# A two-layer conditioned network on one core: the first block's call re-ordered, and a third feed-forward layer whose rounding moves from VectorE to ScalarE

## The chip, the cores and the metric

The kernel runs on one core of one Trainium2 chip. The metric is the device time of one execution in microseconds (us), taken as the median of three runs. The engines are TensorE (PE in the views, with its weight loads as PEld), VectorE (DVE), ScalarE (ACT), GpSimd (POOL) and SyncE (SP, which here only issues DMAs). Each engine runs its own instructions in order, and they meet through semaphores.

## What is computed

```
x = L0_attn_x                                   # [8 sequences, 512 tokens, 128]
sa, ca, ga, sb, cb, gb = split(silu(L0_c) @ L0_wmod)
h = layernorm(x) * (1 + ca) + sa
x = x + ga * L0_attn(h)     # layernorm(ssm(h @ Wp + bp) @ Wo + bo + h) * gamma + beta
h = layernorm(x) * (1 + cb) + sb
x = x + gb * L0_ffn(h)
    # g = silu(h @ w1 * s1) * (h @ w2 * s2)     128 -> 512
    # g = gelu(g @ h1 * s); g = gelu(g @ h2 * s)  512 -> 512, twice
    # return g @ w3 * s3                        512 -> 128
# then the same with block L1: a gated linear attention, and a mixture of LoRA experts
```

The weights `w1, w2, h1, h2, w3` of the first feed-forward network hold only -1, 0 and 1. `ssm` is a linear recurrence over the 512 tokens with 32 states. Only block L0, the function `front` of the kernel, is touched by the change.

## The kernel before

`front` works on the eight sequences in four pairs. A pair `i` has two slots `s`. Its feed-forward network is 24 tiles `j` (the list `TILES`): `j` 0 to 7 are the gated first layer (two products, `gate` and `up`, for each 128 of the 512 hidden columns and each slot), 8 to 15 the first gelu layer (`k` = 1), 16 to 23 the second gelu layer (`k` = 2, the third layer of the network). A tile of a gelu layer is eight 128x512 matmuls into one PSUM bank: four pieces of the 512 hidden rows, and for each one product with the high part of the activations (`hi`, rounded to the type fp32r) and one with the low part (`lo`, the remainder). L1042 is the product with `hi`, L1043 that with `lo`. Gate, up and gelu results take four of the eight PSUM banks in a ring; the other work takes the rest. `USES` lists, by hand, which result goes into which bank in which order, and `Claims` makes TensorE wait for the reader of what stood there before.

Each engine's program is written out by hand as well, as a loop over `i` and `j` with side work hung in at fixed tiles. For the sequence `b` the side work is the recurrent block, in this order:

- `moments_in(b)` (DVE: mean and variance of x), `rescale` (POOL: power -0.5), `apply` or `normalise` (the normalised x, `ssm_out`)
- `flip_h` (PE: four transposes), `bring_h` (ACT: scale and shift into `ssm_hT`), `project` (PE, one for a pair), `bring_u` (ACT), `scan` (DVE, the recurrence, one for a pair)
- `z` (PE: output projection plus residual), `moments_out` (DVE), `rescale_shift` (POOL), `normalise_z` (ACT), `add_bias` (POOL), `update` (DVE: x is updated)
- `moments_ffn` (DVE), `rescale` (POOL), `apply_ffn` (DVE), `flip_ffn` (PE), `bring_ffn` (ACT, twice: full and rounded), `low_h` (DVE: the low part)

For the first pair all of this stands in `prepare`, ahead of the first tile; the modulation vectors (`vectors`, of `SOON` and of `LATER`), the rows spread over partitions (`make_diag` and `spread`) and the flag stand there too. The flag says whether the weights are exact in fp32r: ScalarE sums the low halves of the weights (`sum_piece`), VectorE and TensorE make one number of it, and TensorE branches on it into `run(True)` (two products for each piece) or `run(False)`. With these inputs the flag is zero.

`w_hi` is the rounded copy of all weights, made by ScalarE in seven pieces (`high_piece`), and `w_lo` the remainder, made by POOL in seven pieces (`low_piece`, L732), which only `run(False)` multiplies with. ScalarE's first gelu tile waits for all seven (`w_low`).

In layer 0 a tile goes: ScalarE `silu` of gate, VectorE `product` (L574), ScalarE `round_product` (L844), VectorE `lower` (L587). In the layer `k` = 1 ScalarE evaluates the gelu twice from PSUM, once into `hi` (L853) and once in full (L855), and VectorE subtracts (L587). In `k` = 2 ScalarE evaluates it once, VectorE copies it into `hi` (L585) and subtracts (L587).

## Time and profile before

| | |
|---|---|
| median of 3 runs | 633.18 us (632.43 to 634.87) |
| profiled execution, its own time | 634.81 us |
| its span | 633.0 us |
| PE busy | 543.7 us (86%) |
| DVE busy | 414.6 us (66%) |
| ACT busy | 325.0 us (51%) |
| POOL busy | 228.0 us (36%) |

The span runs from the first to the last instruction of one profiled execution; what lies around it is 1.8 us. Busy is the sum of an engine's instruction times. The clock column of a view is the granted TensorE clock as a share of full speed (1.00 is 2.4 GHz, 0.50 is 1.2 GHz). `front` fills the stretch from 0 to about 266 us; the second block follows it.

### The profile page before, as it was taken

What the parts mean: (1) busy time and instruction counts of PE and PEld (TensorE: products, weight loads), DVE (VectorE), ACT (ScalarE), POOL (GpSimd) and SP (SyncE); (2) the same over time, 40 slices, a digit from 0 to 9 for tenths busy, and PEclk for the clock granted to TensorE, in tenths of its full rate; (3) what the DMA queues carried; (4) which work ended last, traced back from release to release, by engine and by line L of the source; (5) the groups of instructions that cost most, each with busy time, mean ns of one, the idle gap of its engine ahead of it and who ended that gap; (6) DMA issues with size and microseconds to landing.
All of it is one profiled execution on the core that took longest, in us unless ns stands there. A gap on an engine that the chain in (4) does not pass through costs nothing. (4 is left out here: it accounts for less than half of the span.)

```text
span 633.0 us, 10177 instructions
## 1 busy us (share of the span) xinstructions
PE 543.7 (86%) x3688; PEld 444.2 (70%) x3688; DVE 414.6 (66%) x1065; ACT 325.0 (51%) x573; POOL 228.0 (36%) x268
## 2 busy tenths in 40 slices
PE   3837879999999999849999999999999627999994
PEld 2523657777778777638788888888888526878873
DVE  4588649867878675436696776869677642656732
ACT  3467453884886785357655455555542003343340
POOL 2388454802001000044364726446461431323311
PEclk9958889999999999959999999999999966999997
DMA  8300000000040000000000000000000000010001
GB/s 306 98 2 1 2 1 1 1 1 2 29 133 0 1 1 1 0 2 0 1 3 2 1 2 2 2 1 2 1 2 2 1 0 1 1 34 17 26 26 34
DMA packets 10209, 11.67 MB, mean 18 GB/s; under 512 B 656, under 2 KB 9040, under 8 KB 10032
## 3 DMA queue, kind: packets, MB, share of 16 engines
q1 hardware_dynamic: 9120, 10.50, 5.1%
q8 instruction: 30, 0.49, 0.3%
q10 hardware_dynamic: 1040, 0.52, 0.3%
q14 instruction: 19, 0.16, 0.1%
HBM read 8.92 MB, written 2.10 MB: 17 GB/s over the span
## 5 line engine op out<-in xcount | busy, mean ns | idle before, releaser
L1042 PE MATMUL bank<-ffn_g_hi,w_hi 128*128 128x512 f32 x288 | 118.5, 411 | 0.1
L1043 PE MATMUL bank<-ffn_g_lo,w_hi 128*128 128x512 f32 x288 | 114.7, 398 | 0.0
L1287 DVE TENSOR_TENSOR_SCAN att_decay<-bank,att_ident 128x512 f32<-128x512 f32 x64 | 77.6, 1213 | 35.2 <-PE bank L1599 35.0
L587 DVE TENSOR_TENSOR ffn_g_lo<-ffn_full,ffn_g_hi 128x512 fp32r<-128x512 f32 x96 | 70.7, 736 | 33.6 <-ACT ffn_full L855 32.2
L1607 PEld LDWEIGHTS bank<-att_qT,att_hT 128*128 128x128 f32 x512 | 66.0, 191 | 5.5 <-issue 2.0
L1607 PE MATMUL bank<-att_qT,att_hT 128*128 128x128 f32 x512 | 68.0, 276 | 0.6 <-DVE att_state L1311 0.6
L1042 PEld LDWEIGHTS bank<-ffn_g_hi,w_hi 128*128 128x128 f32 x288 | 54.5, 189 | 15.3 <-issue 2.6
L1043 PEld LDWEIGHTS bank<-ffn_g_lo,w_hi 128*128 128x128 f32 x288 | 54.6, 190 | 13.3 <-issue 1.2
L855 ACT ACTIVATE ffn_full<-bank,cols 128x512 f32<-128x512 f32 x64 | 44.3, 693 | 35.1 <-PE bank L1043 29.2
L1486 ACT COPY att_qT<-bank 128x512 f32<-128x512 f32 x64 | 37.3, 587 | 44.7 <-PE bank L167 41.5
L1295 DVE TENSOR_TENSOR att_prob<-bank,att_decay 128x512 f32<-128x512 f32 x64 | 42.6, 666 | 21.9 <-issue 20.5
L1389 POOL TENSOR_TENSOR att_vw<-att_v,att_decay 128x128 f32<-128x128 f32 x64 | 25.9, 406 | 69.4 <-DVE att_decay L1287 69.4
L1977 PE MATMUL bank<-l,lora_hid 128*128 128x155 f32 x256 | 35.6, 296 | 0.0
L1042 PE MATMUL bank<-ffn_h_hi,w_hi 128*128 128x512 f32 x64 | 29.2, 457 | 7.1 <-ACT ffn_gate L839 3.0
L1977 PEld LDWEIGHTS bank<-l,lora_hid 128*128 128x128 f32 x256 | 34.2, 189 | 0.0
L711 POOL TENSOR_TENSOR ffn_in_rstd<-ffn_in_var,neg_half 128x4 f32<-128x4 f32 x8 | 10.6, 1323 | 63.5 <-DVE ffn_in_var L491 63.5
L853 ACT ACTIVATE ffn_g_hi<-bank,cols 128x512 fp32r<-128x512 f32 x32 | 22.2, 693 | 18.2 <-PE bank L1043 18.0
L1855 POOL TENSOR_TENSOR lora_h_lo<-lora_hT,lora_h_hi 128x512 fp32r<-128x512 f32 x8 | 10.2, 1270 | 57.0 <-DVE lora_h_hi L1776 57.0
L1358 POOL TENSOR_SCALAR att_var<-att_mv 128x4 f32<-128x4 f32 x8 | 1.9, 232 | 73.7 <-DVE att_mv L1267 73.1
L574 DVE SCALAR_TENSOR_TENSOR ffn_full<-bank,cols,ffn_gate 128x512 f32<-128x512 f32 x32 | 23.5, 743 | 6.7 <-ACT ffn_gate L839 6.7
L165 PE MATMUL bank<-att_h_hi,m_hi 128*128 128x512 f32 x64 | 27.8, 434 | 0.0
L1043 PE MATMUL bank<-ffn_h_lo,w_hi 128*128 128x512 f32 x64 | 26.8, 419 | 0.0
(225 smaller groups left out, 1292.6 us busy)
## 6 DMA issues: line engine op xcount, KB each, us to landing
w_raw<-in_w_all SPq DMA_DIRECT2D x1, 2304.0 KB, 13.3
out<-lora_res SPq DMA_DIRECT2D x8, 256.0 KB, 2.3
x<-in_x SPq DMA_DIRECT2D x3, 512.0 KB, 12.6
wmod<-in_wmod SPq DMA_DIRECT2D x1, 768.0 KB, 6.3
stage<-in_sel SPq DMA_DIRECT2D x1, 640.0 KB, 8.5
v_raw<-in_v_all SPq DMA_DIRECT2D x1, 576.0 KB, 6.0
x<-in_x ACTq DMA_DIRECT2D x1, 512.0 KB, 4.5
w_raw<-in_w_all SPq DMA_DIRECT2D x1, 512.0 KB, 7.0
```

The source lines that it names most:

```text
L165: pe.matmul(acc, w[0], x[0], start=start, stop=False)
L574: dve.scalar_tensor_tensor(out=full[j % 4][:, :], in0=bank("up", i, j)[:, :], scalar=r["w_scale"][:, 1, m:m + 1], in1=gate[j % 2][:, :], o ...
L587: dve.tensor_tensor(lo, full[j % 4][:, :], hi.bitcast(F32), ALU.subtract).then_inc(low, 1)
L855: act.activation(full[j % 4][:, :], ps, ACT.Gelu, scale=scale).then_inc(gelu_ready, 1)
L1042: pe.matmul(acc, w[0], x[0], start=start, stop=False)
L1043: return pe.matmul(acc, w[0], x[1], start=False, stop=stop)
L1287: dve.tensor_tensor_scan(decay[at % ND][:, :], bank("decay", b, k)[:, :], ident4[:, :], 0.0, ALU.mult, ALU.add).then_inc(decay_ready, 1)
L1295: dve.tensor_tensor(prob[k][:, :], bank("score", b, k)[:, :], decay[at % ND][:, :], ALU.mult).then_inc(prob_ready, 1)
L1389: pool.tensor_tensor(vw[s][:, :, hs], v[s][:, :, hs], last.broadcast_to([P, T, DV]), ALU.mult).then_inc(vw_ready, 1)
L1486: act.copy(qT[b % 2][:, k, :], bank("q", b, k)[:, :]).then_inc(q_ready, 1)
L1607: mm = pe.matmul(ps[:, cc], hT[s][:, cc], qT[s][:, k, cc], start=True, stop=True)
L1977: mm = pe.matmul(bank_e[s][t // 2][:, at:at + D + AR], hid[s][:, k, t * P:(t + 1) * P], r["war2"][:, k, :], start=(k == 0 and t % 2 == 0), ...
```

## The change

It re-orders the side work of `front`, and does four other things:

- **Third layer.** For `k` = 2, as for `k` = 1, ScalarE evaluates the gelu twice (into `hi` and in full), and VectorE's copy L585 and its wait are gone.
- **No `w_lo`.** POOL's seven subtractions and the waits for them are gone. `run(False)`, which these inputs don't take, multiplies with the raw fp32 weights instead.
- **Setup.** The DMAs come in another order and in smaller pieces; `loaded_cond` no longer covers `wmod`. The sigmoid comes ahead of the silu. For sequences 0 and 1 z is normalised by VectorE (`centre`: subtract the mean, times the gain; `update_centred`: times rstd, plus x) without ScalarE's `normalise_z`. `spread` multiplies a broadcast column with the identity, so `make_diag` is gone. Gates of the later modulations (`gates_later`) move into layer 0. The flag's reduction on VectorE is gone. TensorE makes the `LATER` vectors between `z(0)` and `z(1)`. Only the first sequence is brought to its first tile in `prepare`; `flip_ffn(1)`, `bring_ffn(1)` and `low_h(1)` stand in layer 0.
- **Loop.** The z of the next pair are made at tiles 8 and 9 of the pair before it, no longer a pair earlier; `z(2)` and `z(3)` thus leave layer 0 of the first pair. Normalising x for sequences 2 to 7 goes from POOL (L722) to ScalarE (`normalise`), two of them in `prepare` and four in the gelu tiles. Preparing the second block's constants moves from the third pair into the fourth.

```diff
-                sp.dma_start(cT[:, :, :], d["cT"]).then_inc(loaded_cond, 16)
                 sp.dma_start(r["cols"][:, :], d["cols"]).then_inc(loaded_cols, 16)
...
+                sp.dma_start(rows[:, :], d["rows"]).then_inc(loaded_rows, 16)
+                sp.dma_start(cT[:, :, :], d["cT"]).then_inc(loaded_cond, 16)
+                sp.dma_start(wmod[:, 0, 0:3, :], d["wmod"][:, 0, 0:3, :]).then_inc(loaded_soon, 16)
+                sp.dma_start(r["cols"][:, :], d["cols"]).then_inc(loaded_cols, 16)
+                load_w(0)
+                load_x(1)
+                load_w(1)
+                load_w(2)
+                sp.dma_start(wmod[:, 0, 3:6, :], d["wmod"][:, 0, 3:6, :]).then_inc(loaded_later, 16)
+                sp.dma_start(wmod[:, 1, :, :], d["wmod"][:, 1, :, :]).then_inc(loaded_later, 16)
...
+                def centre(b):
+                    dve.wait_ge(spread_ready, 1)
+                    for t in range(T):
+                        ins = dve.scalar_tensor_tensor(out=zn[b][:, t, :], in0=bank("z", b)[:, t * P:(t + 1) * P], scalar=n_out["mv"][:, b, t, 0:1], in1=r["gain_attn0"][:, b, :], op0=ALU.subtract, op1=ALU.mult)
+                    ins.then_inc(centred, 1)
+
+                def update_centred(b):
+                    dve.wait_ge(n_out["rstd_ready"], b + 1)
+                    dve.wait_ge(centred, b + 1)
+                    dve.wait_ge(biased, b + 1)
+                    for t in range(T):
+                        ins = dve.scalar_tensor_tensor(out=x_of(b)[:, t, :], in0=zn[b][:, t, :], scalar=n_out["rstd"][:, b, t:t + 1], in1=x_of(b)[:, t, :], op0=ALU.mult, op1=ALU.add)
+                    ins.then_inc(updated, 1)
...
                     hi, lo = (hid[s][k % 2][q][:, m, :] for q in range(2))
                     if k == 0:
                         dve.wait_ge(high, products(i, j))
-                    elif k == 1:
-                        dve.wait_ge(gelu_ready, gelus(i, j))
                     else:
                         dve.wait_ge(gelu_ready, gelus(i, j))
-                        dve.tensor_copy(hi, full[j % 4][:, :]).then_inc(rounded, 1)
-                        dve.wait_ge(rounded, i * N0 + j - 2 * N0 + 1)
                     dve.tensor_tensor(lo, full[j % 4][:, :], hi.bitcast(F32), ALU.subtract).then_inc(low, 1)
...
-                def low_piece(k):
-                    pool.wait_ge(w_high, k + 1)
-                    pool.tensor_tensor(r["w_lo"][:, piece(k)], w_raw[:, piece(k)], r["w_hi"][:, piece(k)].bitcast(F32), ALU.subtract).then_inc(w_low, 1)
...
+                def normalise(b):
+                    act.wait_ge(n_in["shift_ready"], b - 1)
+                    act.wait_ge(mm, full_at("flip", b - 2))
+                    for t in range(T):
+                        ins = act.activation(ssm_out[b % 2][:, t, :], x_of(b)[:, t, :], ACT.Identity, scale=n_in["rstd"][:, b, t:t + 1], bias=n_in["shift"][:, b, t:t + 1])
+                    ins.then_inc(in_normed, 1)
...
                     ps, scale = bank("gelu", i, j)[:, :], r["w_scale"][:, 1 + k, m:m + 1]
-                    if k == 1:
-                        if i == 0 and j == N0:
-                            act.wait_ge(w_low, PIECES)
-                        act.activation(hid[s][1][0][:, m, :], ps, ACT.Gelu, scale=scale)
+                    act.activation(hid[s][k % 2][0][:, m, :], ps, ACT.Gelu, scale=scale)
                     act.wait_ge(low, made(i, j - 4))
                     act.activation(full[j % 4][:, :], ps, ACT.Gelu, scale=scale).then_inc(gelu_ready, 1)
...
+                        if i < 3:
+                            if j in (11, 12):
+                                normalise_z(e + j - 11)
+                            if j in (18, 19):
+                                bring_ffn(e + j - 18)
+                        if i < 2:
+                            if j in (14, 20):
+                                normalise(e + 2 + (j == 20))
+                            if j in (16, 22):
+                                bring_h(e + 2 + (j == 22))
+                            if j == 23:
+                                bring_u(i + 2)
...
+                            if i < 3 and j in (8, 9):
+                                z(claim, e + j - 8)
+                            if i == 0 and j in (11, 12):
+                                spread(claim, j - 9)
+                            if i < 2 and j == 15:
+                                flip_h(claim, e + 2)
+                            if i < 3 and j in (17, 18):
+                                flip_ffn(claim, e + j - 17)
+                            if i < 2 and j == 21:
+                                flip_h(claim, e + 3)
+                            if i < 2 and j == 23:
+                                project(claim, i + 2)
```

In the last two pieces `e` is `2 * i + 2`, the first sequence of the next pair.

The first place is VectorE in the setup, from the flag's number (`w_inexact`) to the low part of the first layer's input (`ffn_h_lo`). Before:

```order
L635 TENSOR_SCALAR w_inexact<-bank 1x1
L554 TENSOR_TENSOR ssm_zn<-ssm_zn,gain_attn 128x512
L557 TENSOR_TENSOR x<-x,ssm_zn 128x512
L483 BN_STATS ffn_in_stats<-x 128x6 x4
L487 BN_AGGR ffn_in_mv<-ffn_in_stats 128x2 x4
L490 TENSOR_SCALAR ffn_in_neg<-ffn_in_mv 128x4
L491 TENSOR_SCALAR ffn_in_var<-ffn_in_mv 128x4
L508 TENSOR_SCALAR ffn_out<-x,ffn_in_mv,ffn_in_rstd 128x128 x8
L542 TENSOR_TENSOR stage<-cols,spread_col 128x512 x2
L562 TENSOR_TENSOR ffn_h_lo<-ffn_h,ffn_h_hi 128x512 x2
```

And in the changed kernel:

```order
L629 TENSOR_SCALAR w_inexact<-bank 1x1
L479 BN_STATS ssm_out_stats<-bank 128x6 x4
L483 BN_AGGR ssm_out_mv<-ssm_out_stats 128x2 x4
L488 TENSOR_SCALAR ssm_out_var<-ssm_out_mv 128x4
L505 TENSOR_SCALAR ffn_out<-x,ffn_in_mv,ffn_in_rstd 128x128 x4
L555 SCALAR_TENSOR_TENSOR ssm_zn<-bank,ssm_out_mv,gain_attn 128x128 x4
L563 SCALAR_TENSOR_TENSOR x<-ssm_zn,ssm_out_rstd,x 128x128 x4
L479 BN_STATS ffn_in_stats<-x 128x6 x4
L483 BN_AGGR ffn_in_mv<-ffn_in_stats 128x2 x4
L488 TENSOR_SCALAR ffn_in_var<-ffn_in_mv 128x4
L578 TENSOR_TENSOR ffn_h_lo<-ffn_h,ffn_h_hi 128x512
L505 TENSOR_SCALAR ffn_out<-x,ffn_in_mv,ffn_in_rstd 128x128 x4
```

The second sequence's output moments now stand here, and one of the two `ffn_h_lo` stands ahead of the second sequence's `apply_ffn`.

The second place is TensorE at the start of the program. Before, up to the first z (L979 and L980):

```order
L991 MATMUL bank<-scT,wmod 128x8 x3
L241 MATMUL bank<-cols,ssm_out 128x128 x8
L1019 MATMUL bank<-rows 64x128
L1022 MATMUL bank<-cols 32x1 x2
L991 MATMUL bank<-scT,wmod 128x8 x9
L970 MATMUL bank<-ssm_hT,cols 32x512 x2
L986 MATMUL bank<-ffn_full,ones 128x512 x2
```

And in the changed kernel, up to the first z:

```order
L964 MATMUL bank<-scT,wmod 128x8 x3
L990 MATMUL bank<-rows 64x128
L994 MATMUL bank<-cols 32x1 x2
L241 MATMUL bank<-cols,ssm_out 128x128 x8
L938 MATMUL bank<-ssm_hT,cols 32x512 x2
L958 MATMUL bank<-cols,spread_col 128x128 x8
```

The nine `LATER` vectors have left the place ahead of the projection, and the two spreads are eight 128x128 products instead of two 128x512 ones.

The third place is ScalarE at tiles 12 to 16 of the first pair. Before (tiles 12 to 16 are the last of five single L855, with two L853 ahead of them):

```order
L853 ACTIVATE ffn_g_hi<-bank,cols 128x512
L855 ACTIVATE ffn_full<-bank,cols 128x512
L795 ACTIVATE ssm_hT<-bank,sa_bo,mod 128x512
L853 ACTIVATE ffn_g_hi<-bank,cols 128x512
L855 ACTIVATE ffn_full<-bank,cols 128x512
L853 ACTIVATE ffn_g_hi<-bank,cols 128x512
L855 ACTIVATE ffn_full<-bank,cols 128x512
L801 ACTIVATE ssm_u<-bank,b_bias,rows 64x512
L853 ACTIVATE ffn_g_hi<-bank,cols 128x512
L855 ACTIVATE ffn_full<-bank,cols 128x512 x5
```

And in the changed kernel, around tiles 14 to 16:

```order
L770 COPY bias_attn<-bank 128x512
L746 ACTIVATE ssm_out<-x,ssm_in_shift,ssm_in_rstd 128x128 x4
L815 ACTIVATE ffn_g_hi<-bank,cols 128x512
L817 ACTIVATE ffn_full<-bank,cols 128x512
L815 ACTIVATE ffn_g_hi<-bank,cols 128x512
L817 ACTIVATE ffn_full<-bank,cols 128x512
L758 ACTIVATE ssm_hT<-bank,sa_bo,mod 128x512
```

The four short L746 stand between the gelus of tile 14 and tile 15, and the pairs of gelus go on through the third layer.

## Rows read from the trace of the kernel before

**Rows 1.** Stretches: length, busy PE, PEld, DVE, ACT, POOL, clock, DMA, GB/s.

```profile
44.20:70.70 26.50, 19.62 (x76) 13.95 (x77) 23.78 (x46) 18.00 (x27) 19.99 (x11) 0.79 0.00 1
70.70:118.50 47.80, 42.18 (x196) 32.59 (x195) 31.83 (x115) 26.23 (x49) 28.07 (x28) 0.96 0.00 1
118.50:169.20 50.70, 49.50 (x238) 38.73 (x237) 39.34 (x98) 35.91 (x59) 10.62 (x11) 1.00 0.00 1
169.20:215.50 46.30, 45.29 (x209) 36.06 (x208) 36.20 (x79) 34.92 (x54) 2.90 (x2) 1.00 0.17 56
```

**Rows 2.** The timeline of the setup: start, length, engine, line, operation, idle before it.

```profile
8.54 0.22 ACT L860 ACTIVATE scT<-cT 128x16 f32<-128x16 f32 x1 [6.01 <-DMA wmod<-in_wmod]
...
11.11 2.14 DVE L508 TENSOR_SCALAR ssm_out<-x,ssm_in_mv,ssm_in_rstd 128x128 f32<-128x128 f32 x8
...
15.17 4.01 PE L991 MATMUL bank<-scT,wmod 128*128 128x8 f32 x18
...
19.11 1.92 PE L970 MATMUL bank<-ssm_hT,cols 128*32 128x512 f32 x4
...
20.96 3.78 PE L986 MATMUL bank<-ffn_full,ones 128*128 128x512 f32 x4
...
22.05 1.22 DVE L548 TENSOR_TENSOR_SCAN ssm_state<-lam_col,ssm_u 64x512 f32<-64x512 f32 x1 [3.42 <-ACT ssm_u L801]
...
24.54 0.43 PE L979 MATMUL bank<-cols,ssm_hT 128*128 128x128 f32 x2
...
26.57 0.89 DVE L483 BATCH_NORM_STATS2 ssm_out_stats<-bank 128x6 f32<-128x128 f32 x4 [2.20 <-PE bank L980]
...
34.38 0.87 DVE L483 BATCH_NORM_STATS2 ffn_in_stats<-x 128x6 f32<-128x128 f32 x4
...
35.85 0.14 DVE L635 TENSOR_SCALAR w_inexact<-bank 1x1 int32<-1x1 f32 x1
...
40.80 1.94 PE L241 MATMUL bank<-cols,ffn_out 128*128 128x128 f32 x8 [9.37 <-DVE ffn_out L508]
...
44.28 0.77 PE L1042 MATMUL bank<-ffn_h_hi,w_hi 128*128 128x512 f32 x1 [1.54 <-issue]
```

**Rows 3.** One DMA of the start: size in KB, us from issue to landing.

```profile
rows<-in_rows SPq DMA_DIRECT2D x1, 48.8 KB, 3.9
```

**Rows 4.** The timeline of the first pair's layer 0: DVE and POOL.

```profile
60.31 6.73 POOL L732 TENSOR_TENSOR w_lo<-w_raw,w_hi 128x768 fp32r<-128x768 f32 x3
60.53 2.16 DVE L587 TENSOR_TENSOR ffn_g_lo<-ffn_full,ffn_g_hi 128x512 fp32r<-128x512 f32 x1
...
62.61 2.82 DVE L548 TENSOR_TENSOR_SCAN ssm_state<-lam_col,ssm_u 64x512 f32<-64x512 f32 x1
```

**Rows 5.** The timeline of PE where the first gelu tiles of the first two pairs begin.

```profile
65.48 0.72 PE L979 MATMUL bank<-cols,ssm_hT 128*128 128x128 f32 x2 [4.08 <-DVE ssm_state L548]
...
70.71 0.48 PE L1042 MATMUL bank<-ffn_g_hi,w_hi 128*128 128x512 f32 x1
...
130.63 0.48 PE L1042 MATMUL bank<-ffn_g_hi,w_hi 128*128 128x512 f32 x1
...
132.58 0.40 PE L1042 MATMUL bank<-ffn_g_hi,w_hi 128*128 128x512 f32 x1
```

**Rows 6.** PE's waits from 70 to 120 us: total, times, longest.

```profile
PE bank L241 <- POOL ssm_out L722: 3.5, 1, 3.5
PE bank L979 <- DVE ssm_state L548: 1.3, 1, 1.3
```

**Rows 7.** Groups of front's instructions: busy, mean ns, idle before, releasers.

```profile
L587 DVE TENSOR_TENSOR ffn_g_lo<-ffn_full,ffn_g_hi 128x512 fp32r<-128x512 f32 x96 | 70.7, 736 | 33.6 <-ACT ffn_full L855 32.2
...
L855 ACT ACTIVATE ffn_full<-bank,cols 128x512 f32<-128x512 f32 x64 | 44.3, 693 | 35.1 <-PE bank L1043 29.2 <-DVE ffn_g_lo L587 5.9
...
L585 DVE CAST ffn_g_hi<-ffn_full 128x512 fp32r<-128x512 f32 x32 | 13.7, 428 | 15.1 <-ACT ffn_full L855 15.0
```

**Rows 8.** One stretch after that wait of 3.5 us, columns as in rows 1.

```profile
82.70:86.10 3.40, 3.40 (x12) 2.60 (x11) 0.00 (x0) 0.48 (x1) 3.40 (x5) 0.50 0.00 0
```

More of the change, by code:

```diff
@@ L1120, in _ @@
+                    y(PAIRS - 1, 1)
+                    for b in (B - 2, B - 1):
+                        flip_y(claim, b)
                 claim = Claims()
```

580 lines of the change are left out of this document (256 added, 324 removed).

## The prediction

> **What bounds the kernel now.** I read the stretches first, cut where a pair's first tile begins on TensorE [rows 1]. From the second pair on, TensorE is busy for 49.50 of 50.70 us and 45.29 of 46.30: there it is the bound, and what the other engines save is worth nothing as long as they keep up. The two stretches ahead of that are different. From 44.20 to 70.70, the first pair's layer 0, TensorE is busy for 19.62 of 26.50 us, at a mean clock of 0.79, while VectorE is busy for 23.78. The first pair's gelu tiles, 70.70 to 118.50, hold idle time too. And before 44.28 no product of the feed-forward network has started at all [rows 2]. The second block follows, and the change does not touch it. So I look for the gain in three places ahead of 118.50, and for losses in what TensorE has to do or to wait for behind it.
>
> The setup was read in the timeline, as a chain backwards from 44.28 [rows 2]. The reader is to see: the silu waits 6.01 us for the DMA of `wmod`; the nine LATER vectors take 4.01 us on TensorE ahead of the projection; z starts at 24.54; z's first bank is read at 26.57, 2.0 us later; then two sequences go one after the other through VectorE, POOL and ScalarE, up to the transposes at 40.80.
>
> **The setup, step by step.** (a) The silu no longer waits for `wmod`. It now stands behind the sigmoid, which needs `rows`; that DMA is issued first and takes 3.9 us [rows 3], so nothing can be earlier than about 4.6. I take 6.5 for the silu, between 4.6 and 8.54: minus 2.0, bounds minus 3.9 and 0. (b) The LATER vectors leave the place ahead of the projection: minus 3.9 (they fill TensorE's queue from 15.17 to 19.11, and the projection behind them could have run). (c) The first sequence's `apply` (1.07 us, half of L508's 2.14) now stands ahead of the modulations instead of behind them and the gates, so the transposes start sooner: minus 1.4, by that `apply` and a little of the gates; bounds 0 and minus 2.1. Between the projection and z nothing gets shorter: the two spreads hold TensorE for 3.8 us, from 20.96, which is longer than `bring_u` and the scan (over at 23.27). The eight 128x128 products that replace them stream the same number of columns. So z(0) starts at 24.54 - 2.0 - 3.9 - 1.4 = 17.2.
>
> (d) From there I count forward. z(0) 2.0, to 19.2. VectorE: moments 1.5 (34.38 to 35.85), to 20.7, then `centre`. It has no row; four 128x128 operations of the same engine, as in `apply`, are 1.07 us, and I take 1.1 for it and for `update_centred`, with the two passes they replace as the other bound (1.4 together for 128x512 twice; so 0.7 to 1.4 each). That gives 21.8. Meanwhile TensorE makes the LATER vectors, 4.0 us as in the row, or half of it if the clock is up by then; I take 3.0, to 22.2, and VectorE waits for them. Modulations 0.2 (two operations like the 0.14 of 35.85), `update_centred` 1.1, moments 1.5: 25.0. The flag's number and the second sequence's moments 1.6: 26.6. `apply_ffn(0)` 1.1: 27.7. The second sequence's centre, update and moments 3.7: 31.4. `low_h(0)` 0.7, a subtraction like L587 [rows 7]: 32.1. Transposes and `bring_ffn` go beside it: from 40.80 to 44.28 they took 3.5 us with `low_h` in it, so 2.8 without; from 27.7 they are over at 30.5, ahead of `low_h`. The first product then starts at about 32, against 44.28: **minus 12.2**, bounds minus 9 and minus 14.5. TensorE's branch is the one cost without a row: the flag is written at 35.85 and the transposes start at 40.80, so it is anywhere from 0 to 4.9 us. With 4.9 the first product would be at 33.3, which lies within the bounds.
>
> **Layer 0 of the first pair.** Before it takes 26.4 us (44.28 to 70.71). Two things leave it. z(2) and z(3) fill TensorE from 65.48 to 70.71, 5.2 us [rows 5], and they were waited for (4.08 us, for a scan). And POOL's subtractions are gone. The rows show what these did [rows 4]: while L732 ran, a subtraction took 2.16 us and the scan 2.82, where the same subtraction has a mean of 0.74 over the whole of `front` [rows 7] and the scan took 1.22 in the setup [rows 2]. What comes in: `bring_ffn(1)` on ScalarE, `low_h(1)` and `gates_later` on VectorE (0.7, and six operations on few columns, at 0.14 to 0.2 each about 1). Four of five pieces of `w_hi` go out. For the result I take the nearest whole layer: the second pair's runs from 118.50 to 130.63, 12.1 us, with no `low_piece` beside it [rows 1, 5]. To that I add ScalarE's extra work that it lacks (at the 0.69 us of a 128x512 evaluation [rows 7]: `bring_ffn` 1.4, two `bring_h` 1.4, `bring_u` 0.7, a piece of 768 columns 1.0 in proportion, less one `bring_y` 0.7: 3.8), and take off 0.9, a part of what TensorE spent there on output products of the pair before: 15.0. So **minus 11.4**; bounds 13 us and 18 us for the layer, the upper one if TensorE, which starts it after an idle stretch, runs most of it at the lower clock level.
>
> The Trainium skill, page "SBUF — State Buffer", section "Who interferes with whom", bears on this: a VectorE instruction with two SBUF inputs, or in a mode with two ports, is blocked for the whole of a GpSimd instruction that reads SBUF. By this rule the long VectorE instructions go with L732, and the layer falls as above. Without it they'd stay long, and the layer would only lose its 5.2 us of z.
>
> **The first pair's gelu tiles**, 47.8 us. Gone are the waits of 3.5 us for POOL's normalise and of 1.3 us for a scan [rows 6] and the stretch at half clock that followed the first, 3.40 us at 0.50, which costs 1.7 [rows 8]. The z of sequences 4 and 5 are replaced by those of 2 and 3, even. New waits: `flip_h` stands after tiles 15 and 21, and `normalise` on ScalarE behind the gelus of 14 and 20. After the tile's end ScalarE needs two evaluations (1.3 us) and four of 128x128. These have no row for x as the input; together they are at least one 128x512 evaluation, 0.7, and at most four, 2.8; I take 1.5, nearer to the lower end as the columns are the same. So 2.8 us, while the next tile gives TensorE 1.9 us of work (130.63 to 132.58) [rows 5]: 0.9 us of wait each, bounds 0.1 and 2.2, and in the first pair 0.7 more for a `spread`; the projection after tile 23 waits 0.3 more. Together 2.8. z(2) may wait up to 1 for its scan; I take 0.4. Sum: -6.5 + 3.2 = **minus 3.3**.
>
> **Behind it.** The third pair gets two z that it did not have: **plus 3.6** (1.8 each: the first one's 2.0 in the setup, less the handing over to its reader). The second pair gets the same waits of `normalise`: **plus 2.2**. The constants' work moves from the third to the fourth pair, even. The double gelu: 32 more evaluations, at 0.69 us or a little less where they follow each other, on ScalarE, 32 copies of 0.43 us off VectorE [rows 7]. In the second pair ScalarE is busy for 35.91 of 50.70 us; with 8 more gelus (5.5) and two `normalise` (3.0) it is at 44.4. It fits, so I cost it at nothing; TensorE's products hide it. If that cover went, each would cost up to 0.69, 22 in all.
>
> **The sum.** -12.2 - 11.4 - 3.3 + 3.6 + 2.2 = -21.1. The profiled execution took 634.8 us, which is 1.6 above the median; I take the difference to the median, 633.2 - 21.1 = 612.1, and forecast 612.
>
> **Rivals.**
> - *More in front* (0.09): the silu near 4.6, LATER at the higher clock and layer 0 in 13 us: -2, -1 and -2 more, and TensorE never waits for `normalise` because it lags anyway (-4): about 603.
> - *VectorE stays slow in layer 0* (0.10). The long instructions might come from something else than L732, or layer 0 now ping-pongs between three engines with TensorE at half clock. Then the layer loses only z, 21.2 us instead of 15.0: 618. For it speaks that the new layer holds more side work of ScalarE; against it, that the long ones all lie beside POOL's spans.
> - *The setup hardly gains* (0.06). LATER's DMA now stands behind all weights in SP's queue and has no row; before, the whole of `wmod` had landed at 8.54 from the fourth place. If it came at 24 instead of before 19, all that follows would be 5 later: 617, with layer 0's trouble 622.
> - *Slower than before* (0.03): ScalarE becomes the bound of the gelu tiles. The place is the wait for tile j-4's reader on TensorE's ring. It decides when ScalarE needs over 1.9 us a tile throughout: at 1.3 and an average of 0.5 of side work it is at 1.8, so that idle time and then the half clock of rows 8 would come in. A gelu tile at half clock is 1.9 us longer; from 12 of the 64 on, the gain is gone, and with 24 the time is about 657.
> - *The change doesn't do what it says* (0.01): the flag sends TensorE into the fp32 branch. In that type a 128x512 product takes 0.9 us and more (3.78 us for the two spreads [rows 2]) where the gelu tiles have eight in 1.9: some 700 products would be 0.7 us longer each, and the time over 1,000. It sums the same low halves as before, so nothing speaks for it.
>
> **Chances.** The forecast itself, 605 to 617, gets 0.71. The range of 603 to 619 holds it and the near halves of the first three rivals. What a measurement of this kernel can tell from no change is about 0.5%, 3.2 us. Faster by more than that: 0.95; within it 0.01, from the edge of the third rival; slower 0.04, from the last two.
>
> **What the new profile would show.** The silu's ACTIVATE near 6.5; the first z near 17; the first 128x512 product near 32; the first gelu product near 47, and no VectorE instruction of over 1.5 us beside it; waits of about 1 us of the transposes L241 for `ssm_out` from ScalarE, four of them, in place of the 3.5 from POOL; pair starts of TensorE about 91, 144 and 194; the last product of `front` near 245 instead of 266. I am wrong if TensorE waits for ScalarE in the third layer, if the first z waits for LATER's DMA, or if the clock column falls in the gelu tiles.

## The result, and the profile after

The changed kernel takes 619.1 us (median of 4 runs, 618.3 to 619.4) where the kernel before, on the same chip, takes 634.0 (632.4 to 635.5): a ratio of 0.976, 95% interval 0.973 to 0.979. The forecast was 612, with a range up to 619. So the direction and most of the size were right, but the time is 7 us above the forecast, at the very edge of the range. The profiled execution took 619.1 us with a span of 616.8, against a span of 633.0 before: 16.2 less.

The stretches of the changed kernel, from the first product of each pair to that of the next (columns as in [rows 1]; the first line is the setup, the second the first pair's layer 0, the third its gelu tiles, then the second, third and fourth pairs, and the second block):

```profile
0.00:30.90 30.90, 15.54 (x100) 12.09 (x101) 22.72 (x119) 19.07 (x30) 12.93 (x22) 0.91 0.64 208
...
30.90:44.90 14.00, 13.08 (x48) 9.11 (x49) 11.99 (x23) 11.07 (x19) 2.29 (x2) 0.83 0.00 1
44.90:89.20 44.30, 40.93 (x205) 32.40 (x205) 28.93 (x94) 36.91 (x66) 11.24 (x12) 1.00 0.00 1
89.20:145.80 56.60, 51.67 (x237) 39.55 (x236) 37.43 (x107) 43.09 (x75) 10.70 (x12) 0.97 0.00 1
145.80:197.20 51.40, 47.67 (x225) 37.71 (x224) 34.17 (x87) 38.18 (x64) 5.55 (x6) 1.00 0.15 50
197.20:250.60 53.40, 51.50 (x249) 40.94 (x247) 26.85 (x40) 42.10 (x68) 0.00 (x0) 1.00 0.00 1
250.60:616.80 366.20, 317.79 (x2683) 271.28 (x2680) 227.00 (x556) 157.35 (x298) 146.36 (x188) 0.94 0.02 7
```

Against [rows 1] the first pair is far shorter (layer 0 by 12.4, the gelu tiles by 3.5), but the second pair is 5.9 us longer, and TensorE is now idle in it for 4.9 us where before it was idle for 1.2. The third grew by 5.0 (from 46.4 to 51.4 by TensorE's starts), the fourth by 2.6.

The setup on ACT, PE and DVE (columns as in [rows 2]):

```profile
5.76 0.22 ACT L825 ACTIVATE scT<-cT 128x16 f32<-128x16 f32 x1
...
6.54 1.42 PE L964 MATMUL bank<-scT,wmod 128*128 128x8 f32 x6 [6.54 <-DMA wmod<-in_wmod]
...
10.75 1.96 PE L938 MATMUL bank<-ssm_hT,cols 128*32 128x512 f32 x4
12.64 2.05 PE L958 MATMUL bank<-cols,spread_col 128*128 128x128 f32 x16
15.03 0.46 PE L947 MATMUL bank<-cols,ssm_hT 128*128 128x128 f32 x2 [0.34 <-issue]
...
17.88 2.17 PE L964 MATMUL bank<-scT,wmod 128*128 128x8 f32 x18 [0.83 <-DMA wmod<-in_wmod]
...
22.85 0.14 DVE L629 TENSOR_SCALAR w_inexact<-bank 1x1 int32<-1x1 f32 x1
...
24.31 1.11 DVE L505 TENSOR_SCALAR ffn_out<-x,ffn_in_mv,ffn_in_rstd 128x128 f32<-128x128 f32 x4
...
27.52 1.09 PE L241 MATMUL bank<-cols,ffn_out 128*128 128x128 f32 x4 [5.36 <-issue]
...
30.92 0.77 PE L1019 MATMUL bank<-ffn_h_hi,w_hi 128*128 128x512 f32 x1 [2.31 <-issue]
```

The first product starts at 30.92 instead of 44.28. TensorE's waits from 45 to 262 us, in which the changed loop lies (columns as in [rows 6]; a wait of 8.5 us that belongs to the second block is left out):

```profile
...
PE bank L241 <- ACT ssm_out L746: 6.9, 4, 1.8
PE bank L1019 <- ACT ffn_gate L804: 2.7, 3, 0.9
PE bank L241 <- DVE ffn_out L505: 2.4, 1, 2.4
```

Four waits of `flip_h` for ScalarE's `normalise` have taken the place of the one for POOL [rows 6], as forecast in number, but at 1.5 to 1.8 us and not 0.9. The view counts a wait from the modelled end of the last product, and products overlap by 0.15 us; what TensorE loses is 0.15 more, and from here on I call that the gap: 1.66, 1.99, 1.83 and 2.00 us for the four. A wait of 2.4 us for VectorE in `flip_ffn`, in the third pair, was not forecast. Here is what ScalarE does ahead of the last of the four (timeline of ACT; L815 and L817 are the two gelus, L247 `bring_ffn`, L746 `normalise`), and TensorE's answer:

```profile
129.19 0.69 ACT L815 ACTIVATE ffn_g_hi<-bank,cols 128x512 fp32r<-128x512 f32 x1 [1.34 <-PE bank L1020]
129.78 0.68 ACT L817 ACTIVATE ffn_full<-bank,cols 128x512 f32<-128x512 f32 x1
130.35 0.78 ACT L247 ACTIVATE ffn_h_hi<-bank,mod 128x512 fp32r<-128x512 f32 x1
131.01 0.79 ACT L247 ACTIVATE ffn_h<-bank,mod 128x512 f32<-128x512 f32 x1
131.68 0.70 ACT L815 ACTIVATE ffn_g_hi<-bank,cols 128x512 fp32r<-128x512 f32 x1
132.25 0.71 ACT L817 ACTIVATE ffn_full<-bank,cols 128x512 f32<-128x512 f32 x1
132.82 0.81 ACT L247 ACTIVATE ffn_h_hi<-bank,mod 128x512 fp32r<-128x512 f32 x1
133.48 0.82 ACT L247 ACTIVATE ffn_h<-bank,mod 128x512 f32<-128x512 f32 x1
134.14 0.73 ACT L815 ACTIVATE ffn_g_hi<-bank,cols 128x512 fp32r<-128x512 f32 x1
134.72 0.74 ACT L817 ACTIVATE ffn_full<-bank,cols 128x512 f32<-128x512 f32 x1
135.29 1.68 ACT L746 ACTIVATE ssm_out<-x,ssm_in_shift,ssm_in_rstd 128x128 f32<-128x128 f32 x4
...
137.02 0.66 PE L241 MATMUL bank<-cols,ssm_out 128*128 128x128 f32 x4 [1.85 <-ACT ssm_out L746]
```

From 129.19 on ScalarE never stops: a tile with two gelus and a `bring_ffn` takes it 2.5 us (129.19 to 131.68, then to 134.14), while TensorE makes a tile in 1.9. Two such tiles in a row put it 1.2 us behind, and `normalise` stands at the end of that queue. 1.0 us behind the wait the granted clock falls, from 1.00 to the lower of the two levels (1.2 GHz), for 3.4 us as in [rows 8]; that costs 1.7 us more:

```profile
137.80:141.20 3.40, 3.40 (x10) 2.69 (x9) 0.73 (x1) 0.79 (x2) 0.54 (x1) 0.53 0.00 0
```

### The profile page after: what moved, and what is told of

Read it like the earlier page. It is cut to its first block and busy times, and to the rows that moved or that the text cites. A ratio compares the mean times of both kernels' runs of the same rounds, so it can differ in the third digit from the quotient of the medians.

```text
span 616.8 us, 10227 instructions
## 1 busy us (share of the span) xinstructions
PE 538.2 (87%) x3740; PEld 443.1 (72%) x3740; DVE 389.1 (63%) x1023; ACT 347.8 (56%) x618; POOL 189.1 (31%) x241
## 5 line engine op out<-in xcount | busy, mean ns | idle before, releaser
L599 DVE TENSOR_TENSOR ffn_g_lo<-ffn_full,ffn_g_hi 128x512 fp32r<-128x512 f32 x96 | 66.0, 688 | 61.3 <-ACT ffn_full L817 60.9
L1463 ACT COPY att_qT<-bank 128x512 f32<-128x512 f32 x64 | 37.4, 588 | 44.4 <-PE bank L167 41.2
L815 ACT ACTIVATE ffn_g_hi<-bank,cols 128x512 fp32r<-128x512 f32 x64 | 44.9, 702 | 30.6 <-PE bank L1020 29.8
L817 ACT ACTIVATE ffn_full<-bank,cols 128x512 f32<-128x512 f32 x64 | 44.8, 699 | 0.0
L696 POOL TENSOR_TENSOR ssm_out_rstd<-ssm_out_var,neg_half 128x4 f32<-128x4 f32 x8 | 9.2, 1155 | 86.4 <-DVE ssm_out_var L488 86.4
L1886 ACT CAST lora_zT<-bank 96x512 fp32r<-96x512 f32 x16 | 9.2, 577 | 33.9 <-PE bank L1931 33.9
L1899 ACT ACTIVATE lora_hid<-bank 128x512 f32<-128x512 f32 x32 | 19.1, 598 | 13.9 <-PE bank L1945 13.9
## 6 DMA issues: line engine op xcount, KB each, us to landing
x<-in_x SPq DMA_DIRECT2D x3, 512.0 KB, 12.4
```

The costliest lines, as they stand in the source:

```text
L599: dve.tensor_tensor(lo, full[j % 4][:, :], hi.bitcast(F32), ALU.subtract).then_inc(low, 1)
L815: act.activation(hid[s][k % 2][0][:, m, :], ps, ACT.Gelu, scale=scale)
L817: act.activation(full[j % 4][:, :], ps, ACT.Gelu, scale=scale).then_inc(gelu_ready, 1)
L1463: act.copy(qT[b % 2][:, k, :], bank("q", b, k)[:, :]).then_inc(q_ready, 1)
```

## The experiments

Theory A: what is missing was lost by ScalarE running late for `flip_h` at tiles 14 and 20, in part through the double gelu, and by VectorE running late for `flip_ffn`. Rival B: the double gelu is free, and the engines would only trade one wait for another. To compare them apart from the setup, whose length varies from run to run (first product at 30.4 to 33.6 us), I give "the loop": from the first product of the first pair to the last of the fourth, in the profiled execution. It is 218.1 us in the changed kernel and 220.5 before.

| kernel | time, us | ratio to before, 95% | loop, us |
|---|---|---|---|
| changed, again | 619.0 | 0.974 (0.972 to 0.976) | 218.3 |
| gelu only (on before) | 641.3 | 1.010 (1.007 to 1.014) | 227.3 |
| gelu, not last four tiles (on before) | 635.5 | 1.001 (0.999 to 1.003) | 221.1 |
| no w_lo (on before) | 626.9 | 0.986 (0.982 to 0.990) | 214.5 |
| no w_lo, moments later (on before) | 630.1 | 0.992 (0.989 to 0.995) | 217.6 |
| copy back (on changed) | 615.5 | 0.968 (0.964 to 0.973) | 215.1 |
| normalise on POOL | 614.5 | 0.968 (0.964 to 0.973) | 212.8 |
| ffn flips later | 622.0 | 0.981 (0.978 to 0.984) | 217.5 |
| normalise on POOL, ffn flips later | 610.5 | 0.963 (0.960 to 0.967) | 208.9 |
| normalised flips later | 611.4 | 0.963 (0.959 to 0.967) | 210.0 |
| both flips later | 607.6 | 0.956 (0.954 to 0.959) | 206.7 |
| both later, copy back | 607.2 | 0.956 (0.954 to 0.959) | 205.0 |

**The changed kernel again**, without any edit.

> The changed kernel itself once more, to stand beside the others of this call: 618 to 620 us, ratio to the kernel before 0.974 to 0.979, the four waits for ssm_out and the one for ffn_out where they were.

It came as expected, with the same five waits to 0.02 us. What follows is thus read against steady waits. But the half clock is not steady: here it is absent behind the wait at tile 21 and stands behind the one for `ffn_out` instead, which ends at 181.36 (windows of this run):

```profile
137.80:141.20 3.40, 3.40 (x16) 2.38 (x16) 1.22 (x2) 2.17 (x4) 0.00 (x0) 1.00 0.00 0
182.70:186.10 3.40, 3.40 (x12) 2.76 (x11) 0.88 (x3) 1.34 (x3) 0.00 (x0) 0.51 0.81 242
```

So the second pair takes 55.3 us here instead of 56.6, and the third 53.0 instead of 51.4, with the same program. Where a single drop of the clock stands says nothing of an edit.

**The double gelu alone**, in the kernel before:

```diff
-                    if k == 1:
-                        ...
-                        act.activation(hid[s][1][0][:, m, :], ps, ACT.Gelu, scale=scale)
+                    ...
+                    act.activation(hid[s][k % 2][0][:, m, :], ps, ACT.Gelu, scale=scale)
...
-                        dve.tensor_copy(hi, full[j % 4][:, :]).then_inc(rounded, 1)
-                        dve.wait_ge(rounded, i * N0 + j - 2 * N0 + 1)
```

> The kernel before, with the one edit of the third layer: ScalarE evaluates the gelu twice, VectorE's copy is gone. Theory (VectorE's chain bounds no gelu tile, ScalarE has room): within 0.3% of the kernel before, 632 to 635 us; ScalarE's busy time rises by about 96 evaluations of 0.45 us in all (as many as the copies that go), VectorE's falls by about 40 us, and TensorE's waits for a gelu product's input change by under 1 us in all. Rival: ScalarE is the later of the two in these tiles, and waits of the product L1042 for ffn_gate grow by 3 us or more: 636 to 645 us.

The theory fails: it is 6.8 us slower than the kernel before. The time lies in the rival's range, but its mechanism is only half there, as the waits for `ffn_gate` grow by 1.9 us in all (2.7 to 4.6) and not by 3. (The edit adds 32 evaluations and not 96: ScalarE's busy time rises by 17.8 us and VectorE's falls by 12.4.) The cost isn't spread over the tiles. 4.6 us of it fall in the second pair's layer 0, 16.7 us here and 12.1 in the kernel before. There VectorE's last `update` of the pair begins 0.8 us later (120.19 against 119.41) and POOL's `add_bias` 1.8 us sooner (119.76 against 121.53), so that they meet (windows of layer 0; then the timelines of DVE and of POOL):

```profile
117.90:134.60 16.70, 13.73 (x48) 9.59 (x47) 13.38 (x18) 12.03 (x21) 5.17 (x4) 0.80 0.00 0
...
118.43 0.69 DVE L557 TENSOR_TENSOR x<-x,ssm_zn 128x512 f32<-128x512 f32 x1
...
120.19 1.75 DVE L554 TENSOR_TENSOR ssm_zn<-ssm_zn,gain_attn 128x512 f32<-128x512 f32 x1
122.04 1.59 DVE L557 TENSOR_TENSOR x<-x,ssm_zn 128x512 f32<-128x512 f32 x1
...
119.76 3.31 POOL L724 TENSOR_TENSOR x<-x,bias_attn 128x512 f32<-128x512 f32 x2
```

The same two instructions that take 0.68 and 0.69 a tile earlier take 1.75 and 1.59 here; TensorE then waits 1.9 us for `ffn_gate` and 1.0 for `ffn_full`, and runs on at half clock for 6.8 us (mean 0.80 over the layer). At the start of the third pair the wait for `ffn_gate` is 1.9 us as well, in place of 0.9, with no such meeting and no drop of the clock, and that pair is 1.3 us longer. So about 1.3 us a time is ScalarE's lateness by itself, and the rest of the second pair's loss the meeting and the clock.

**The same, but the copy kept in tiles 20 to 23.**

```diff
-                    if k == 1:
+                    if j < 20:
-                        act.activation(hid[s][1][0][:, m, :], ps, ACT.Gelu, scale=scale)
+                        act.activation(hid[s][k % 2][0][:, m, :], ps, ACT.Gelu, scale=scale)
```

> The kernel before with ScalarE's double evaluation in tiles 16 to 19 of the third layer, and VectorE's copy kept in tiles 20 to 23. Theory (the 5.5 us of span that the double evaluation alone cost came from the pair's end, where ScalarE's last evaluations and two normalisations pile up, so that the second pair's layer 0 began late, ran into GpSimd's add_bias and the half clock): layer 0 of the second pair takes 12.1 to 12.5 us again in place of 16.7, and the time is within 1.5 us of the kernel before. Rival (the cost is spread over the tiles, half of it is left): 2.5 us or more over the kernel before.

The time is that of the kernel before, as the theory had it; the layer is back at 12.1 us with the clock at 1.00, and the third pair at its 46.4:

```profile
118.00:130.10 12.10, 11.09 (x51) 8.05 (x50) 11.35 (x18) 10.74 (x18) 6.10 (x5) 1.00 0.00 1
```

So in tiles 16 to 19 the double gelu costs nothing that can be measured. In this order it costs where ScalarE's result is due at once: at a pair's end.

**The copy back in the changed kernel.**

```diff
+                        dve.tensor_copy(hi, full[j % 4][:, :]).then_inc(rounded, 1)
+                        dve.wait_ge(rounded, i * N0 + j - 2 * N0 + 1)
...
-                    act.activation(hid[s][k % 2][0][:, m, :], ps, ACT.Gelu, scale=scale)
+                    if k == 1:
+                        act.activation(hid[s][1][0][:, m, :], ps, ACT.Gelu, scale=scale)
```

> The changed kernel, with VectorE's copy of the third layer back and ScalarE evaluating that gelu once. Theory A (TensorE's longer waits for the flip of a normalised sequence at tiles 14 to 15 and 20 to 21 come from ScalarE's backlog of double evaluations): the four waits for L746 (6.9 us in all in the changed kernel) fall to under 4 us, the stretch at half clock at 137.8 us goes, and the time is 3 to 4.5 us under the changed kernel's (about 615 to 616 us). Rival B (VectorE is then the later one): the wait of flip_ffn for ffn_out (L505, 2.4 us) grows and the product L1019 waits more for L590: no gain, or slower by up to 3 us.

615.5 us, as theory A had it: 3.6 less than the changed kernel (the four runs go from 613.5 to 617.3). TensorE's waits:

```profile
PE bank L241 <- ACT ssm_out L750: 4.2, 4, 1.7
...
PE bank L241 <- DVE ffn_out L505: 2.4, 1, 2.4
```

The gaps at tile 21 fall from 1.99 and 2.00 to 0.65 and 0.66; those at tile 15 stay at 1.66 and 1.83, since in tiles 8 to 15 the gelu was evaluated twice before too, and what delays ScalarE there are two `normalise_z` of 1.5 us. Theory A also had the half clock at 137.8 go. It does, but one stands behind the wait for `ffn_out`, where the changed kernel's second profile has it too:

```profile
180.00:182.00 2.00, 2.00 (x7) 1.53 (x6) 1.97 (x7) 0.00 (x0) 0.00 (x0) 0.61 0.92 328
182.00:184.00 2.00, 2.00 (x8) 1.69 (x7) 0.98 (x3) 1.64 (x3) 0.00 (x0) 0.54 0.00 0
```

So no gain at the clock is shown. Read against that second profile, whose drop stands at the same place, the copy back takes 1.6 us off the first pair, 1.6 off the second and nothing off the third.

**The normalise of sequences 4 to 7 on POOL.**

```diff
+                def normalise(b):
+                    pool.wait_ge(mm, full_at("flip", b - 2))
+                    for t in range(T):
+                        ins = pool.tensor_scalar(ssm_out[b % 2][:, t, :], x_of(b)[:, t, :], n_in["rstd"][:, b, t:t + 1], n_in["shift"][:, b, t:t + 1], ALU.mult, ALU.add)
+                    ins.then_inc(in_normed, 1)
...
-                            if j in (14, 20):
-                                normalise(e + 2 + (j == 20))
```

> The changed kernel, with the normalise of sequences 4 to 7 on GpSimd, right behind their statistics, in place of ScalarE. Theory A (ScalarE's backlog at tiles 14 and 20 is what makes TensorE wait for the flip): the four waits for ssm_out, 6.9 us with 7.5 us of gaps, are gone or under 0.5 us each, the clock stays up at 137.8 us, and the time is about 8 us under the changed kernel's: 610 to 612. Rival B: GpSimd's pass over shared memory lengthens VectorE's instructions beside it or ends late itself; the waits stay over 1 us each, now for GpSimd, or the wait of flip_ffn for ffn_out grows by 2 us or more per pair: 615 to 622.

614.5 us, between the two. Three of the four waits are gone, one stays (now for POOL, in the second pair), new ones of 0.3 us for `ffn_out` come in the first two pairs, and the half clock stands behind the `ffn_out` wait of 2.4 us in the third:

```profile
PE bank L241 <- DVE ffn_out L505: 3.1, 3, 2.4
...
PE bank L241 <- POOL ssm_out L706: 1.5, 1, 1.5
```

**`flip_ffn` one tile later** (the flips after tiles 18 and 19, `bring_ffn` at 19 and 20, `low_h` at 20 and 21).

```diff
-                            if j in (18, 19):
-                                bring_ffn(e + j - 18)
+                            if j in (19, 20):
+                                bring_ffn(e + j - 19)
...
-                            if i < 3 and j in (17, 18):
-                                flip_ffn(claim, e + j - 17)
+                            if i < 3 and j in (18, 19):
+                                flip_ffn(claim, e + j - 18)
```

> The changed kernel, with flip_ffn, its copy back and the rounding behind it one tile later in pairs 0 to 2. Theory A (the wait of 2.4 us in the third pair is VectorE's apply ending late, and a tile more covers it): that wait falls to 0.5 us or less, but the copy back at tile 20 now stands ahead of ScalarE's normalise at tile 20 in the first two pairs and lengthens those two waits by up to 1.3 us each: net 0 to -2 us, 617 to 619. Rival B: no wait moves and the low part comes late for the next pair's layer 0: +1 to +3 us, 620 to 622.

The waits moved as A says: the one for `ffn_out` from 2.4 to 0.5, the two at tile 21 up by 0.7 each, to gaps of 2.70. The loop is 0.6 shorter; the time, 622.0, is nevertheless 3 longer than the changed kernel's. In the profiled execution 0.9 of that is a longer setup and 2.0 the second block, neither of which the edit touches. The changed kernel's second profile has a second block as long (1.7 us more than the first profile), but its median is still 619.0. The time lies in B's range without B's mechanism, as the waits did move. What the 3 us are is not explained.

**Both: POOL's normalise, and `flip_ffn` one tile later.**

> Both edits: the normalise of sequences 4 to 7 on GpSimd, and flip_ffn with its copy back one tile later. Theory A: the two gains add, since GpSimd's normalise no longer stands behind the copy back on ScalarE: 8 us + 2.4 us, about 608 to 610 us. Rival B: GpSimd lengthens VectorE's chain that ends in flip_ffn's input, and the tile more only just pays for it: 611 to 616.

610.5, half a microsecond above A's range. The loop is 9.2 us shorter; left are the one wait for POOL (1.5) and 0.5 for `ffn_out`, and the clock stays at 1.00 in all four pairs' gelu tiles.

**The flips of normalised sequences one tile later** (after 16 and 22, `bring_h` a tile later too, projection in the next pair's layer 0), ScalarE as in the changed kernel.

```diff
-                            if i < 2 and j == 15:
+                            if i < 2 and j == 16:
                                 flip_h(claim, e + 2)
...
-                            if i < 2 and j == 21:
+                            if i < 2 and j == 22:
                                 flip_h(claim, e + 3)
-                            if i < 2 and j == 23:
-                                project(claim, i + 2)
```

> The changed kernel, with the two flips of normalised sequences one tile later (after tiles 16 and 22 in place of 15 and 21), the copies back one tile later, and projection and its copy in the next pair's layer 0. Theory A (the waits are only a matter of ScalarE's normalise ending 1.8 us after the flip is due, a tile being about 1.9 us): the four waits of 1.7 to 2.0 us fall to 0.2 each, the clock does not drop at 137.8 us (1.7 us more), and the time is 7 to 8 us under the changed kernel's: about 611 to 612. Rival B: the copy back and the projection then come late for the next pair's z and scan in its layer 0, and half or more is given back there as a new wait of z or u: 615 to 618.

611.4, as A expected, though not by its mechanism alone. All four waits are gone, no drop of the clock stands in the gelu tiles, and the projection makes no new wait. In their place `flip_ffn` now waits in each of three pairs, for 5.0 us in all: 0.6 and 2.0 in the first two, where TensorE reaches it sooner by a wait that is gone, and the 2.4 of the third pair that was there before:

```profile
PE bank L241 <- DVE ffn_out L505: 5.0, 3, 2.4
```

**Both flips later, and then with the copy back.**

> The changed kernel, with both pairs of flips one tile later: those of normalised sequences (after tiles 16 and 22, projection in the next pair's layer 0) and flip_ffn (after tiles 18 and 19), each with its copy back and rounding behind it. Theory (the waits are each a matter of a step that ends 0.8 to 2.6 us after its flip is due, and do not move elsewhere): the three gaps that are left with only the first edit (0.77, 2.10 and 2.56 us, for ffn_out) fall to 0.7 in all, about 4.5 us less than that run's 607.5 us span: span 603, time 605 to 607. Rival (the low part then comes late for the next pair's layer 0, or ScalarE's copy back at tile 20 delays the normalise at 20 past its flip at 22): half is given back, time 608 to 611.

> The same with VectorE's copy of the third layer back, ScalarE evaluating that gelu once. Theory (the double evaluation costs only through ScalarE's lateness for a flip or at a pair's end; where the flips have room it is free): the same time as the kernel without the copy, within 1.5 us. Rival A (it costs by itself, a little in every tile): 3 us or more faster. Rival B (VectorE's chain to apply_ffn is then the later one): 1.5 to 4 us slower, with waits for ffn_out L505 back.

607.6 and 607.2 us: the same within their spread, some 12 us under the changed kernel and 28 under the one before. With the double gelu two gaps of 0.83 us for `ssm_out` at tile 22 are left, with the copy none; that is the 1.7 us between their loops. So where the flips have a tile more, the double gelu is close to free. The pairs of the faster one (gelu tiles of the first pair, then the second and the third pair):

```profile
45.20:84.50 39.30, 39.27 (x202) 32.32 (x201) 32.51 (x101) 31.68 (x57) 12.25 (x12) 1.00 0.00 1
84.50:134.90 50.40, 49.65 (x238) 38.29 (x237) 41.65 (x115) 38.68 (x67) 11.74 (x12) 1.00 0.00 1
134.90:184.70 49.80, 48.60 (x229) 37.68 (x228) 39.06 (x98) 34.53 (x57) 5.55 (x6) 1.00 0.15 52
```

In the first pair's gelu tiles TensorE is busy for 39.27 of 39.30 us: nothing is left to take from waits there.

**What layer 0 of the first pair gained from.** Two kernels made from the one before. First, POOL's subtractions left out, with the waits for them. `run(False)` reads the raw weight in place of the low part, but these inputs don't take it: every product that runs is the same as before.

```diff
-                def low_piece(k):
-                    ...
-                    pool.tensor_tensor(r["w_lo"][:, piece(k)], w_raw[:, piece(k)], r["w_hi"][:, piece(k)].bitcast(F32), ALU.subtract).then_inc(w_low, 1)
...
-                    return r["w_hi"][:, at:at + P], r["w_lo"][:, at:at + P]
+                    return r["w_hi"][:, at:at + P], w_raw[:, at:at + P]
```

> The kernel before without GpSimd's work on the low part of the weights (w_lo): the products read the raw weight in its place, so the second matmul of each pair is taken in plain float32 arithmetic with the unrounded weight, which changes what the low product adds; number and size of instructions stay. Theory of the prediction (the 5 to 7 us instructions of VectorE in layer 0 of the first pair, rows 4, are long because GpSimd's w_lo runs beside them): VectorE's apply (L732) falls from 6.73 to about 3 us and layer 0 of the first pair shrinks by 4 to 7 us of its 26.4. Rival: they stay over 5 us, and layer 0 shrinks by 1 us or less. How long the changed product takes is not known, so the reading is VectorE's instructions in the first 70 us, not the whole time.

The text above calls L732 VectorE's and speaks of instructions of 5 to 7 us; [rows 4] has it as POOL's subtraction, gone here, and VectorE's long ones as 2.16 and 2.82. The size came as expected: layer 0 falls from 26.4 to 20.1 us, and the two instructions are back at 0.68 and 1.21:

```profile
43.40:63.50 20.10, 16.73 (x76) 11.46 (x77) 16.68 (x41) 17.69 (x27) 5.58 (x5) 0.89 0.00 2
...
58.06 0.68 DVE L587 TENSOR_TENSOR ffn_g_lo<-ffn_full,ffn_g_hi 128x512 fp32r<-128x512 f32 x1
58.66 1.21 DVE L548 TENSOR_TENSOR_SCAN ssm_state<-lam_col,ssm_u 64x512 f32<-64x512 f32 x1
```

So it was the overlap with L732: those 6.3 us go with it, 4.7 of them as a shorter hold at the z, whose scan is ready sooner.

The Trainium skill, page "SBUF — State Buffer", section "Who interferes with whom", says that a VectorE instruction with two SBUF inputs contends with a GpSimd instruction that reads SBUF. This run and the double-gelu run agree with it.

Then the statistics of sequences 4 and 5 moved besides, to tiles 9 and 10 (and POOL's work on sequences 2 and 3 ahead of that on 4 and 5, to match):

```diff
-                    for b in (4, 5):
-                        moments_in(b)
...
+                            if j in (9, 10):
+                                moments_in(j - 5)
```

> The kernel before without GpSimd's w_lo (the products read the raw weight in its place, as in the earlier run of that edit), and besides with VectorE's statistics of sequences 4 and 5 moved from ahead of the first product of layer 0 to tiles 9 and 10. Theory (the 20.1 us that layer 0 of the first pair still took stood 2.9 us of statistics ahead of VectorE's first product, the rest is the half clock and the steps of the setup that run over into it): layer 0 of that pair takes 16.5 to 18 us. Rival (VectorE was waiting for ScalarE's gates anyway): within 1 us of 20.1.

Layer 0 takes 18.5 us, 1.6 less, at the theory's upper edge: VectorE starts its first product 2.7 us sooner after TensorE's but then waits 1.2 for ScalarE's next gate. And the whole is 3 us slower, since `normalise` on POOL now ends late: TensorE's wait for it is 8.0 us in place of the 3.5 of [rows 6].

```profile
PE bank L241 <- POOL ssm_out L722: 8.0, 1, 8.0
```

The other 4.5 us down to the changed kernel's 14.0 no run isolates, but the trace shows a term of that size: z(2) and z(3) still stand in this layer in both kernels and hold the products up for 4.8 us, 1.0 of it a wait for the scan. In the trace without `w_lo`, the last product ahead of them, the first of the z and the first product behind:

```profile
58.53 0.40 PE L1034 MATMUL bank<-ffn_h_lo,w_hi 128*128 128x512 f32 x1
59.92 0.49 PE L969 MATMUL bank<-cols,ssm_hT 128*128 128x128 f32 x2 [0.99 <-DVE ssm_state L548]
...
63.52 0.47 PE L1033 MATMUL bank<-ffn_g_hi,w_hi 128*128 128x512 f32 x1
```

In the changed kernel they stand in the gelu tiles. Four pieces of `w_hi` (0.85 us each) are no longer between ScalarE's gates either; what those are worth is not shown.

## Why the prediction held in front and failed behind

Its terms against what was measured (starts of TensorE's pairs in both traces):

| term | forecast | measured |
|---|---|---|
| setup | -12.2 | -13.4 |
| layer 0 of the first pair | -11.4 | -12.4 |
| gelu tiles of the first pair | -3.3 | -3.5 |
| second pair | +2.2 | +5.9 |
| third and fourth pair | +3.6 | +7.6 |
| second block | 0 | -0.4 |
| sum | -21.1 | -16.2 |

That 619.1 stands at the range's edge and not beyond it is luck: the three terms in front came out 1.2, 1.0 and 0.2 us better than forecast and took back part of what the ones behind lost. With the front as forecast the time would have been over 621. Two of the signs that the prediction named for being wrong are there: TensorE waits for ScalarE in the third layer (1.8 us at tile 21, twice), and the clock falls in the gelu tiles once. (One sum among the rivals is off: 617 with layer 0's 6 us is 623, not 622. Nothing rests on it.)

**Setup: right in sum, by terms that cancel, and tested by no run.** The silu came at 5.76, not 6.5; the spreads, which I had left at 3.8 us, took 2.05, and LATER 2.17 where I took 3.0. The second wait for `wmod` was only 0.83. So z(0) started at 15.03 instead of 17.2, and `apply_ffn(0)` was over at 25.4 instead of 27.7. The transposes started only at 27.52: TensorE's branch, the cost without a row that the sum left out, took back 2.1 us. All this is read from the trace; no run takes a step of the setup out.

**Layer 0: right, with half of its cause shown.** Half of the 12.4 is L732's overlap (6.3, the run without w_lo); the statistics that stood ahead are 1.6, and z(2) and z(3), which the prediction had leave with 5.2 us, account for the other 4.5 by the trace. The length, 14.0 us, lies in the bounds of 13 to 18.

**The first pair's gelu tiles: right in sum.** The waits for `normalise` were 1.67 and 1.99 us instead of 0.9 each, but the clock stayed up and there was no wait for the scan.

**The second pair: mis-sized, 2.2 against 5.9.** The step that failed is the price of `normalise`: two evaluations and four of 128x128 from the tile's end on, so 2.8 us, while the next tile gives TensorE 1.9. That supposes an idle ScalarE at the tile's end. It had a queue of 0.8 to 1.2 us, from two `normalise_z` or two `bring_ffn` in the tiles ahead. The gaps became 1.83 and 2.00, 4.0 us longer in all than the flips without a wait, and the clock fell once behind the second, another 1.7 that the sum had at nothing. (In the second profile of the same kernel that 1.7 stands in the third pair.)

**The double gelu: "it fits, so I cost it at nothing" failed.** The sum over a pair, 44.4 of 50.7 us, was right in size (43.1 of 56.6 measured) and says nothing of tiles 18 and 19, in which ScalarE has 2.5 us of work per 1.9, with `normalise` right behind. The copy back gives 3.6 us in this order, of which 2.7 are the two gaps at tile 21. That it is hardly a cost by itself, the two kernels with both flips later show, and the one that keeps the copy in the last four tiles only.

**The third and fourth pair: a wait that I didn't look for.** Two z at 1.8 us each are 3.6, as forecast. 2.6 more is `flip_ffn` waiting for VectorE's `apply_ffn`, and 0.5 goes in each layer 0; 0.4 of the 7.6 is not assigned. The constants' 1.8 us moved from the third pair to the fourth, even as forecast. I had followed the new work on ScalarE and not VectorE's chain to `apply_ffn`; one tile later the wait is 0.5 instead of 2.4.

Of the rivals, "slower" names the right engine, but ScalarE never was the bound throughout.

## What to carry to other kernels

An engine's mean load over a stage doesn't say whether extra work on it is free. List, tile by tile, what it has to do in the two or three tiles ahead of each result that another engine waits for, and add the queue that is left to the result's own length; here four flips moved by one tile each were worth 7.6 us (a drop of the clock among them), and taking a quarter of ScalarE's gelus away was worth 3.6. A gain in front of a pipeline that is paced by hand-placed steps lets the bound engine arrive earlier at each of them, so that waits appear that no edit made: look at every such step for what is late next.

## What the runs showed of the hardware

- The granted clock doesn't fall behind every gap of the same length, and not even behind the same gap of the same program. In the changed kernel's first profile a gap of 2.00 us that ends at 137.02 is followed by 3.4 us at half clock and one of 2.57 that ends at 183.22 by full clock. In its second profile the same two gaps (ends 136.47 and 181.36) have it the other way round. With the flips of the normalised sequences later, gaps of 2.11 and 2.57 us in one profile are followed by full clock. A drop of 3.4 us costs 1.7, but its price can be put on a run, not on a single wait.
- From the end of the flag's write (22.99) to TensorE's first instruction behind the branch (27.52) 4.5 us go by, shown as "issue", and the data was ready 2.1 us earlier. In eight of the nine profiled runs with this branch order it is 4.4 to 4.7 us, in the ninth 5.9. How much of it is the branch itself, no run separates.
- VectorE and POOL don't slow each other evenly. Beside POOL's `tensor_tensor`, with two inputs in SBUF, VectorE's with two inputs in SBUF ends a little behind the end of POOL's: L587 at 62.69 where L732's first ends at 62.13, and in the double-gelu run L554 at 121.94 and L557 at 123.63 where the two of L724 end at 121.39 and 123.07, so 0.55 or 0.56 us each. L574, one of whose two inputs lies in PSUM, takes its 0.72 us beside L732 as well. Beside POOL's `normalise` in the kernel before, a `tensor_scalar` with one such input besides its scalars (eight of L722 in 10.13 us from 111.42, where its median is 0.85 each), VectorE's L554 takes 0.68 us and it is POOL that is stretched, to 1.78. The Trainium skill's page "SBUF — State Buffer", same section, says that the order of issue, and not the form of the operation, decides who blocks. By the starts in the traces this doesn't tell the two apart: POOL's instruction starts first in both (119.76 against 120.19, 116.38 against 116.90). Whether the form does, no run here tests.
- With the same setup, the first product starts anywhere from 30.4 to 31.8 us in eight of nine profiled runs of the changed kernel and those made from it, and at 33.6 in one, the one with the 5.9 us at the branch, so that a profiled span alone can't settle a difference of 2 us.
